# One expert per 32-column tile in the first layer of a mixture of experts

## The chip, the cores and the metric

The kernel runs on one core of a Trainium2 chip. The metric is the time in microseconds of one execution, the median of three runs. Lower is better. A core has TensorE (matmuls, which write into PSUM, 8 banks of 128 partitions x 512 f32), VectorE, ScalarE, GpSimd (POOL) and SyncE (SP), each with an instruction stream of its own; they wait for each other with semaphores.

## The reference

```
x = x + tanh(g_xattn) * xattn(layernorm(x), ctx)           # 16 batches, 1024 tokens, 512 features
x = x + tanh(g_ffn) * ffn(layernorm(x))
ffn:   grouped = x.reshape(b, s // 32, 32, d)              # 32 groups of 32 tokens
       logits  = einsum('bntd,des->bntes', grouped, Wc) + bc + tie     # 32 x 4 = 128 experts
       perm    = (logits == max over the 32 tokens)        # each expert takes one token of each group
       permuted        = einsum('bntd,bntes->bnesd', grouped, perm)    # the gather
       inner           = relu(einsum('bnesd,esdf->bnesf', permuted, W1) + b1)   # first layer, 512 -> 32
       result_permuted = einsum('bnesf,esdf->bnesd', inner, W2) + b2            # second layer, 32 -> 512
       result          = einsum('bnesd,bntes->bntd', result_permuted, perm)     # the scatter
```

Each of the 128 experts has its own W1 (512 x 32) and takes 32 tokens of a batch, one from each of the 32 groups.

## The kernel before

The program has two parts that follow each other. The attention part handles 32 half batches and leaves its result in `out`. The expert part (`experts`, from L1074) then goes through 16 batches, and the change touches only this part. It runs in f32.

TensorE's order for batch i stands in `tensor`. There is first one stretch, the **gather and first layer**: pieces n = 0 to 7, each one block of 128 features (n // 2) for one half of the tokens or of the experts (n % 2). `gather(i, n)` (L1398) picks tokens with 16 matmuls of 32 rows x 128 columns, four row tiles beside each other, into four banks: banks 4 to 7, or 0 to 3 for n = 1. ScalarE and VectorE copy these banks into `gat` (`copy`, L1285 and L1341). `inner(i, p)` (L1422) then multiplies: for each pair of experts one matmul with 64 columns of W1-side rows, so that the 64x64 result holds the two experts' products with both experts' tokens; half of each result is never used. All pieces add up in banks 0 to 3, which `bias` (L1413) has filled with b1 first. The pieces go in the order gather 0, 1, 2, bias, inner 0, gather 3, inner 1 and so on. In every second batch the pieces are taken in reverse.

Eight `relu` steps on ScalarE (`hidden`, L1291) take the useful quarter-rows of these banks into `hid`. After the stretch TensorE does the scatter of the batch before (`scatter`, 8 tiles), the second layer (`outer`, 8 steps of 4 bias matmuls and 16 matmuls on 32x32 tiles) and two transposes of the choice for the next batch (`route.chosen_T`, L208). ScalarE copies these into `sel` (L213), and the next gather needs them. VectorE's `swap` (L1339) transposes the second layer's result in `res` for the scatter.

Weights that don't stay in SBUF are loaded in quarters of 256 KB: W1 by SP (L1197, L1205), three pieces of W2 by ScalarE's queue (`load_second`, L1185), the last of them after the last piece of the first layer (`m_w1` step 7). POOL normalises the next batch's tiles (`route.normed`, L182) and adds the finished tiles to `out` (L1260); between the first four and the last four tiles it waits for the last W2 load.

Semaphore counts are kept by `Mark` objects; `m_gaA` and `m_gaV` count ScalarE's and VectorE's copies, `m_w1` the pieces of the first layer, `m_hr` the relus.

Of the kernel before, what the change touches and what calls it, by code (L numbers as in the profile page):

```python
# [17 lines left out]
P = 128  # L18
# [3 lines left out]
E, G = 128, 32  # L22
F = 32
# [1044 lines left out]
def experts(nc, top, ps, kept, d_kept, consts, ident, gate_f, xin, ring, d_ring, route, m_b2s, late_logits, logits_landed, w1_dram, w2_dram, out):  # L1068
# [7 lines left out]
    with st:  # L1076
# [19 lines left out]
        m_gaA, m_hr, m_evA = mark("gaA", 2 * C), mark("hr", 8), mark("evA", 8)  # L1096
        m_gaV, m_evV, m_tr, m_fin = mark("gaV", 2 * C), mark("evV", 8), mark("tr", 8), mark("fin", NT - 2)
# [9 lines left out]
        front = lambda n: 0 if n == 1 else 4  # L1107
# [40 lines left out]
        def gathered(n, g):  # L1148

            return (gat[:, n // 2 % 2, :].rearrange("p (e h g t) -> p h e g t", h=2, g=GT, t=TH)[:, n % 2, :, g],  # L1150
                    ps[:, front(n):front(n) + 4, :].rearrange("p g (t e) -> p e g t", t=TH)[:, :, g])
# [132 lines left out]
        def scalar(e):  # L1284
            def copy(i, n):  # L1285
                e.wait_ge(m_gap.sem, m_gap.at(i, n))
                room_for(e, i, n)
                o, v = gathered(n, slice(0, 2 if n < 2 else 3))
                e.activation(o, v, ACT.Copy).then_inc(m_gaA.sem, 1)  # L1289

            def hidden(i, j, p):  # L1291
                e.wait_ge(m_w1.sem, m_w1.at(i, p))
                o, v = relu(i, j, piece(i, p) % 2)
# [7 lines left out]
            for i in range(B):  # L1301
                if live(i):
# [31 lines left out]
        def vector(e):  # L1334
# [6 lines left out]
            def copy(i, n):  # L1341
                e.wait_ge(m_gap.sem, m_gap.at(i, n))
                room_for(e, i, n)
                o, v = gathered(n, slice(2 if n < 2 else 3, 4))
# [216 lines left out]
```

## Time and profile before

| | us |
|---|---|
| median of 3 runs | 1759.36 (1754.37 to 1762.72) |
| the profiled execution | 1774.67 |
| its span | 1772.9 |
| attention part, about | 0 to 884 |
| sixteen stretches of gather and first layer, in sum | 485.2 |

| engine | busy us | share |
|---|---|---|
| TensorE, matmuls | 1638.3 | 92% |
| TensorE, weight loads | 1147.6 | 65% |
| VectorE | 1296.2 | 73% |
| POOL | 854.9 | 48% |
| ScalarE | 736.4 | 42% |

The mean granted clock of TensorE is 0.979 of full speed. Matmuls overlap each other and the weight loads, so the busy time of TensorE is that of the union of its records, whose ends are modelled. The chain of waits that ended last is TensorE's for 57%, DMA's for 19%, VectorE's for 12%; for 5% of the span it holds "issue", time in which an engine waited for nothing that the profile shows.

### The profile page before, as it was taken

How to read it: one execution, taken by the hardware profiler on the slowest of the kernel's cores; microseconds unless marked ns; L12 is line 12 of the kernel's file. 1: busy time of each engine (PE TensorE's matmuls, PEld its weight loads, DVE VectorE, ACT ScalarE, POOL GpSimd, SP SyncE). 2: the span in 40 equal slices, each digit the busy share in tenths (PEclk: the TensorE clock that was granted, in tenths of full speed). 3: DMA queues.
4: the chain of work that ended last, by engine and by line, in shares of the span. 5: the costliest groups of instructions: out<-in, count | busy, mean ns of one | idle time of the engine just before them, and what ended most of it. 6: DMA issues, size and time to landing. Idle time of an engine off the chain costs nothing.

```text
span 1772.9 us, 51861 instructions
## 1 busy us (share of the span) xinstructions
PE 1638.3 (92%) x22488; PEld 1147.6 (65%) x22488; DVE 1296.2 (73%) x1886; ACT 736.4 (42%) x965; POOL 854.9 (48%) x1016
## 2 busy tenths in 40 slices
PE   7899999999999999999878999999988989998995
PEld 4677777777777777777656555666555666554663
DVE  5677777787777777777717777677777777776866
ACT  3532323233332333233234555454555554555552
POOL 3368777877778777877611222122222122222122
PEclk9999999999999999999989999999999999999997
DMA  7634545554454545454554887777888777878765
GB/s 273 171 98 148 172 142 176 156 164 159 148 189 159 167 145 177 155 165 148 185 188 141 214 216 212 210 204 201 223 212 213 214 209 198 208 204 226 213 170 157
DMA packets 180882, 324.81 MB, mean 183 GB/s; under 512 B 23344, under 2 KB 33328, under 8 KB 179248
## 3 DMA queue, kind: packets, MB, share of 16 engines
q1 hardware_dynamic: 135728, 239.68, 42.5%
q0 software_dynamic: 17280, 31.46, 11.0%
q10 hardware_dynamic: 27648, 50.34, 8.9%
q8 instruction: 179, 2.93, 0.7%
q14 instruction: 47, 0.39, 0.1%
HBM read 242.71 MB, written 78.71 MB: 181 GB/s over the span
## 4 chain that ended last, share of the span: by engine, by line
PE 57%; DMA 19%; DVE 12%; issue 5%; ACT 3%; POOL 2%; SPq 1%; ACTq 0%; POOLq 0%; DVEq 0%
PE ps L1435 12%; PE ps L899 10%; PE ps L946 10%; DMA xin<-out 7%; PE ps L1408 6%; DMA out<-xin 5%; PE ps L959 5%; PE ps L914 3%; PE ps L972 3%; DVE mx L694 2%; DMA gat<-in_W 2%; PE ps L1459 2%; DMA sel<-lg_scratch 2%; PE ps L933 2%; ACT lg L663 2%
## 5 line engine op out<-in xcount | busy, mean ns | idle before, releaser
L182 POOL TENSOR_SCALAR xin<-xin,r_all,nb_all 128x512 f32<-128x512 f32 x128 | 112.2, 880 | 524.7 <-DMA xin<-out 377.4
L1339 DVE STREAM_TRANSPOSE res<-res 128x2048 f32<-128x2048 f32 x128 | 292.1, 2295 | 0.1
L1289 ACT ACTIVATE gat<-ps 128x1536 f32<-128x1536 f32 (+1 forms) x128 | 170.9, 1344 | 235.4 <-PE ps L1408 235.2
L1355 DVE COPY res<-ps 128x1024 f32<-128x1024 f32 x128 | 156.7, 1225 | 85.3 <-PE ps L1459 66.2
L899 PE MATMUL ps<-xTh,qh 128*128 128x512 f32 x512 | 209.5, 409 | 5.0 <-DVE qs L711 1.4
L1408 PE MATMUL ps<-sel,xin 32*128 32x128 f32 x4096 | 157.2, 284 | 51.0 <-issue 25.7
L899 PE MATMUL ps<-xTh,ql 128*128 128x512 f32 x512 | 200.8, 392 | 0.0
L899 PE MATMUL ps<-xTl,qh 128*128 128x512 f32 x512 | 200.3, 391 | 0.0
L1345 DVE COPY gat<-ps 128x512 f32<-128x512 f32 (+1 forms) x128 | 104.1, 816 | 102.6 <-PE ps L1408 102.4
L1408 PEld LDWEIGHTS ps<-sel,xin 32*128 32x128 f32 x4096 | 131.9, 186 | 65.5 <-issue 38.9
L1299 ACT ACTIVATE res<-ps 128x1024 f32<-128x1024 f32 x128 | 131.0, 1024 | 101.0 <-PE ps L1459 90.4
L530 POOL TENSOR_TENSOR xTl<-xT,xTh 128x512 fp32r<-128x512 f32 x128 | 160.4, 1284 | 11.2 <-ACT xTh L595 11.2
L1260 POOL DMA_DIRECT2D out<-xin x120 | 119.0, 1049 | 95.8 <-DVE xin L1174 80.2
L946 PE MATMUL ps<-vw,pTh 128*128 128x512 f32 x512 | 164.2, 402 | 0.1
L543 POOL TENSOR_TENSOR qc<-qc,qs 128x512 f32<-128x512 f32 x64 | 82.8, 1294 | 162.9 <-DVE qs L711 162.9
L726 DVE TENSOR_TENSOR xin<-ps,xin 128x512 f32<-128x512 f32 x128 | 88.2, 689 | 67.2 <-PE ps L946 67.2
L710 DVE TENSOR_TENSOR qc<-ps,cos 128x512 f32<-128x512 f32 x128 | 86.9, 679 | 60.0 <-PE ps L899 59.9
L946 PEld LDWEIGHTS ps<-vw,pTh 128*128 128x128 f32 x512 | 94.1, 189 | 45.6 <-issue 25.2
L612 ACT ACTIVATE lx<-ps 128x512 f32<-128x512 f32 x32 | 19.1, 597 | 245.1 <-PE ps L959 245.1
L899 PEld LDWEIGHTS ps<-xTh,qh 128*128 128x128 f32 x512 | 96.6, 189 | 35.3 <-DVE qs L711 18.1
L663 ACT ACTIVATE lg<-lg,sc 128x256 f32<-128x256 f32 x128 | 58.2, 502 | 133.6 <-DVE lg L698 133.6
L1435 PE MATMUL ps<-gat,kept 128*64 128x64 f32 x3072 | 107.2, 229 | 6.3 <-issue 6.1
(156 smaller groups left out, 3335.2 us busy)
## 6 DMA issues: line engine op xcount, KB each, us to landing
gat<-in_W ACTq DMA_DIRECT2D x192, 256.0 KB, 5.1
xT<-in_xT SPq DMA_DIRECT2D x32, 1024.0 KB, 6.2
xin<-in_x SPq DMA_DIRECT2D x64, 512.0 KB, 3.8
out<-xin SPq DMA_DIRECT2D x64, 512.0 KB, 4.3
xin<-out SPq DMA_DIRECT2D x128, 256.0 KB, 4.1
xin<-in_W SPq DMA_DIRECT2D x128, 256.0 KB, 3.9
out<-xin POOLq DMA_DIRECT2D x120, 256.0 KB, 7.5
xT<-in_W SPq DMA_DIRECT2D x68, 256.0 KB, 4.6
```

The source lines that it names most:

```text
L182: e.tensor_scalar(self.xn[:, t, :], self.xn[:, t, :], self.r[:, i, t:t + 1], self.nb[:, i, t:t + 1], ALU.mult, ALU.add).then_inc(self.m_xn ...
L530: e.tensor_tensor(xTl[:, c, :], xT[:, c, :], xTh[:, c, :].bitcast(F32), ALU.subtract).then_inc(m_lo.sem, 1)
L899: last = e.matmul(ps[:, 2 + n % 2, :], a[:, c, n * DH:(n + 1) * DH], b[:, c, :], start=(k == 0), stop=(k == len(parts) - 1))
L946: last = e.matmul(ps[:, 5 + t % 2, :], a[:, t // 2, column:column + P], vw[:, u // 2 % 2, k, p, :], start=(m == 0), stop=(m == len(parts) ...
L1260: e.dma_start(batch(out, b, t, 1)[:, 0], tile_of(t), accum_op=ALU.add).then_inc(d_ys[t].sem, 16)
L1289: e.activation(o, v, ACT.Copy).then_inc(m_gaA.sem, 1)
L1299: e.activation(o, v, ACT.Copy).then_inc(m_evA.sem, 1)
L1339: e.transpose(v, v).then_inc(m_tr.sem, 1)
L1345: e.tensor_copy(o, v).then_inc(m_gaV.sem, 1)
L1355: e.tensor_copy(o, v).then_inc(m_evV.sem, 1)
L1408: last = e.matmul(ps[:, front(n) + g, t * E:(t + 1) * E], xn[r, h * TH + t, c * P:(c + 1) * P], sel[r, h * TH + t, :], start=True, stop=True)
L1435: last = e.matmul(ps[a * 64:(a + 1) * 64, q // 8, q % 8 * 64:(q % 8 + 1) * 64], first(i, p)[:, (e0 % 64) * F:(e0 % 64 + 2) * F], gat[:, c ...
```

## The change

In `inner` each expert gets a matmul of its own: 32 columns of weights in the column tile j = 0 to 3, its own 32 tokens as the moving rows, a 32x32 result without an unused part. Four column tiles stand beside each other, and 64 matmuls take the place of 32 in a piece. The results of all experts fit two banks (0 and 1) instead of four, so `bias` has two matmuls instead of four and waits for `sel` rather than for the copies, and `relu` has two steps of 128 partitions instead of eight of 32. The six banks 2 to 7 form a ring for the gathers: gather n takes four banks from 2 + (4n mod 6) on. `gathered(n, k)` copies two banks at a time; for n < 2 ScalarE takes the first two and VectorE the last two, as before, and from n = 2 on ScalarE takes both in two steps, where before it took three banks and VectorE one. VectorE's swaps no longer have copies between them, and the first stands ahead of copy 0. Two of the four loads of W2_MOVED[1] and all of W2_MOVED[2] move behind later steps of ScalarE's loop over the finished tiles.

```diff
-        front = lambda n: 0 if n == 1 else 4
+        front = lambda n, g: 2 + (4 * n + g) % 6
...
-        def relu(i, j, h):
-            return (hid(i)[j * F:(j + 1) * F].rearrange("p (s q) n -> p s q n", s=4)[:, 2 * h:2 * h + 2],
-                    ps[j * F:(j + 1) * F, 2 * h:2 * h + 2, :].rearrange("p s (q b n) -> p s q b n", b=2, n=NG)[:, :, :, j % 2])
+        def relu(i, h):
+            return hid(i)[:, h * Q // 2:(h + 1) * Q // 2].rearrange("p q n -> p (q n)"), ps[:, h, :]
...
+        def in_place(e, i, n, k):
+            if n < 2 and k:
+                e.wait_ge(m_gaV.sem, m_gaV.at(i, n))
+            else:
+                e.wait_ge(m_gaA.sem, m_gaA.at(i, n if n < 2 else 2 * n - 2 + k))
...
-                    for p in (2 * C - 2, 2 * C - 1):
-                        for j in range(4):
-                            hidden(i, j, p)
-                            if p % 2:
-                                load_second(e, i, W2_MOVED[1], j)
+                    hidden(i, 2 * C - 2)
+                    hidden(i, 2 * C - 1)
+                    for c in range(2):
+                        load_second(e, i, W2_MOVED[1], c)
...
-                    if live(i) and t < QUARTERS:
-                        load_second(e, i, W2_MOVED[2], t)
+                    if live(i) and t < 2:
+                        load_second(e, i, W2_MOVED[1], 2 + t)
+                    elif live(i) and t < 2 + QUARTERS:
+                        load_second(e, i, W2_MOVED[2], t - 2)
...
-                    if live(i):
-                        if k == 0:
-                            copy(i, 0)
-                        if k < 7:
-                            copy(i, k + 1)
                     if live(i - 1):
                         swap(i - 1, k)
+                    if live(i) and k == 0:
+                        copy(i, 0)
+                        copy(i, 1)
...
+                if n:
+                    in_place(e, i, n - 1, 0)
                 if n >= 2:
-                    k = 0 if n == 2 else n - 1
-                    e.wait_ge(m_gaA.sem, m_gaA.at(i, k))
-                    e.wait_ge(m_gaV.sem, m_gaV.at(i, k))
+                    in_place(e, i, n - 2, 1)
...
-                    for a in range(2):
-                        e0 = 4 * q + 2 * a
-                        last = e.matmul(ps[a * 64:(a + 1) * 64, q // 8, q % 8 * 64:(q % 8 + 1) * 64],
-                                        first(i, p)[:, (e0 % 64) * F:(e0 % 64 + 2) * F], gat[:, c % 2, e0 * NG:(e0 + 2) * NG],
+                    for j in range(4):
+                        e0 = 4 * q + j
+                        last = e.matmul(ps[j * F:(j + 1) * F, q // 16, q % 16 * NG:(q % 16 + 1) * NG],
+                                        first(i, p)[:, (e0 % 64) * F:(e0 % 64 + 1) * F], gat[:, c % 2, e0 * NG:(e0 + 1) * NG],
                                         start=False, stop=(c == C - 1), skip_group_check=True)
```

TensorE at the start of the second batch's stretch, before. `ps<-sel,xin` is a gather, `ps<-ident,b1r` the bias, `ps<-gat,...` a piece of the first layer with its weights in `xT`, `xin` or `kept`; the numbers are the result's shape and how many stand in a row.

```order
L1408 MATMUL ps<-sel,xin 128x128 x48
L1418 MATMUL ps<-ident,b1r 128x512 x4
L1435 MATMUL ps<-gat,xT 64x64 x32
L1408 MATMUL ps<-sel,xin 128x128 x16
L1435 MATMUL ps<-gat,xin 64x64 x32
L1408 MATMUL ps<-sel,xin 128x128 x16
L1435 MATMUL ps<-gat,kept 64x64 x32
```

The same place in the changed kernel:

```order
L1415 MATMUL ps<-sel,xin 128x128 x32
L1424 MATMUL ps<-ident,b1r 128x512 x2
L1415 MATMUL ps<-sel,xin 128x128 x16
L1441 MATMUL ps<-gat,xT 32x32 x64
L1415 MATMUL ps<-sel,xin 128x128 x16
L1441 MATMUL ps<-gat,xin 32x32 x64
L1415 MATMUL ps<-sel,xin 128x128 x16
L1441 MATMUL ps<-gat,kept 32x32 x64
```

The bias stands one gather earlier, and each piece has 64 matmuls in place of 32, between the same gathers.

ScalarE at the end of the second batch's stretch, before: `gat<-in_W` is a load of a quarter of W2, `gat<-ps 32x512` a relu, `xin<-ps,gate_f` a finished tile of the batch before.

```order
L1289 ACTIVATE gat<-ps 128x128x12 x6
L1185 DMA gat<-in_W 128x512 x4
L1294 ACTIVATE gat<-ps 32x512 x5
L1185 DMA gat<-in_W 128x512
L1294 ACTIVATE gat<-ps 32x512
L1185 DMA gat<-in_W 128x512
L1294 ACTIVATE gat<-ps 32x512
L1185 DMA gat<-in_W 128x512
L1294 ACTIVATE gat<-ps 32x512
L1185 DMA gat<-in_W 128x512 x3
L1176 ACTIVATE xin<-ps,gate_f 128x512
L1185 DMA gat<-in_W 128x512
```

And in the changed kernel:

```order
L1297 ACTIVATE gat<-ps 128x128x8 x14
L1192 DMA gat<-in_W 128x512 x4
L1302 ACTIVATE gat<-ps 128x512 x2
L1192 DMA gat<-in_W 128x512 x4
L1183 ACTIVATE xin<-ps,gate_f 128x512
L1192 DMA gat<-in_W 128x512
L1183 ACTIVATE xin<-ps,gate_f 128x512
L1192 DMA gat<-in_W 128x512
```

Fourteen copies of 128x128x8 take the place of two of that size and six of 128x128x12; two relus stand where eight stood; the last load of W2 stands behind the fourth finished tile, where it stood behind the second.

## Rows read from the trace of the kernel before

**Rows 1.** The page: busy us, share and instructions of each engine.

```profile
PE 1638.3 (92%) x22488; PEld 1147.6 (65%) x22488; DVE 1296.2 (73%) x1886; ACT 736.4 (42%) x965; POOL 854.9 (48%) x1016
```

**Rows 2.** TensorE's waits, 780 to 1773 us: us in total, times, longest.

```profile
PE ps L1408 <- issue: 25.7, 22, 2.2
...
PE ps L1435 <- issue: 9.7, 12, 1.7
...
PE ps L1418 <- DVE gat L1345: 5.0, 11, 0.5
...
PE ps L1454 <- ACT gat L1294: 4.5, 1, 4.5
```

**Rows 3.** Busy time by stretch: gather and first layer; the last row a scatter.

```profile
core 0: us, PE busy (x) PEld busy (x) DVE busy (x) ACT busy (x) POOL busy (x), PEclk, DMA share, GB/s
...
1049.40:1080.00 30.60, 26.97 (x780) 24.42 (x784) 24.20 (x16) 12.75 (x12) 5.29 (x7) 1.00 0.71 191
1102.20:1137.00 34.80, 30.03 (x780) 27.49 (x784) 24.84 (x17) 12.80 (x12) 5.18 (x7) 0.90 0.63 180
...
sum 485.20, PE 432.85 PEld 393.20 DVE 373.00 ACT 202.51 POOL 68.23; mean PE 27.05 PEld 24.57 DVE 23.31 ACT 12.66 POOL 4.26
...
1080.00:1087.00 7.00, 7.00 (x69) 1.86 (x68) 4.71 (x7) 6.15 (x11) 3.51 (x4) 1.00 0.94 284
```

**Rows 4.** TensorE in order of time: start, us, what, count, idle before.

```profile
1006.78 0.50 PE L1408 MATMUL ps<-sel,xin 32*128 32x128 f32 x7 [0.90 <-issue]
1007.21 2.08 PE L1435 MATMUL ps<-gat,xin 128*64 128x64 f32 x64
1009.23 1.17 PE L1408 MATMUL ps<-sel,xin 32*128 32x128 f32 x32
1010.33 0.92 PE L1435 MATMUL ps<-gat,kept 128*64 128x64 f32 x24
1011.64 0.74 PE L1435 MATMUL ps<-gat,kept 128*64 128x64 f32 x18 [0.39 <-issue]
```

**Rows 5.** The same view in the batch with the longest stretch.

```profile
1112.81 0.50 PE L1408 MATMUL ps<-sel,xin 32*128 32x128 f32 x6 [2.16 <-issue]
1113.24 3.63 PE L1435 MATMUL ps<-gat,xin 128*64 128x64 f32 x64
...
1126.26 0.94 PE L1408 MATMUL ps<-sel,xin 32*128 32x128 f32 x23
1129.13 0.60 PE L1408 MATMUL ps<-sel,xin 32*128 32x128 f32 x9 [1.92 <-issue]
```

**Rows 6.** 780 to 1773 us: instruction queue (packets, MB, share); instructions of each engine.

```profile
q8 instruction: 149, 2.44, 1.0%
...
780.00:1773.00 993.00, 880.75 (x18833) 576.85 (x18831) 706.74 (x675) 481.64 (x556) 284.85 (x343) 0.97 0.73 198
```

**Rows 7.** TensorE after a wait; then the instruction queue, 1059.65 to 1059.75.

```profile
1058.58 0.50 PE L1408 MATMUL ps<-sel,xin 32*128 32x128 f32 x7 [0.90 <-issue]
...
q8 instruction: 1, 0.02, 71.2%
```

**Rows 8.** The instruction queue, 1110.45 to 1110.55.

```profile
q8 instruction: 1, 0.02, 58.2%
```

**Rows 9.** Last scatter at full clock; matmuls of L1459, 1034.42 to 1034.50.

```profile
1759.31 1.96 PE L1486 MATMUL ps<-res,selT 128*32 128x128 f32 x64 [0.74 <-DVE res L1339]
...
1034.43 0.68 PE L1459 MATMUL ps<-kept,gat 32*32 32x512 f32 x11
```

**Rows 10.** ScalarE by form, 780 to 1773 us: count, busy us, mean ns, idle before.

```profile
L1289 ACT ACTIVATE gat<-ps 128x1536 f32<-128x1536 f32 x96 | 139.3, 1451 | 209.2 <-PE ps L1408 209.0
...
L1289 ACT ACTIVATE gat<-ps 128x1024 f32<-128x1024 f32 x32 | 32.3, 1023 | 26.2 <-PE ps L1408 26.2
```

**Rows 11.** TensorE in order of time: gathers 1 and 2 of a batch.

```profile
1050.95 2.27 PE L1408 MATMUL ps<-sel,xin 32*128 32x128 f32 x64 [0.33 <-POOL xin L182]
```

**Rows 12.** The last load of W2 on ScalarE's queue.

```profile
1031.88 0.78 ACTq L1185 DMA_DIRECT2D gat<-in_W  x1
```

More of the change, by code:

```diff
@@ L1095, in experts @@
         m_gap, m_w1, m_w2, m_sc = mark("gap", 2 * C), mark("w1", 2 * C), mark("w2", 8), mark("sc", NT)
[L1096 to L1097 removed]
+        m_gaA, m_hr, m_evA = mark("gaA", 4 * C - 2), mark("hr", 2), mark("evA", 8)
+        m_gaV, m_evV, m_tr, m_fin = mark("gaV", 2), mark("evV", 8), mark("tr", 8), mark("fin", NT - 2)
         d_last = mark("last", 4, 16)
@@ L1140, in second, with gathered @@
             return v.rearrange("p (k d) -> p k d", d=D)
-        def relu(i, j, h):
-            return (hid(i)[j * F:(j + 1) * F].rearrange("p (s q) n -> p s q n", s=4)[:, 2 * h:2 * h + 2],
-                    ps[j * F:(j + 1) * F, 2 * h:2 * h + 2, :].rearrange("p s (q b n) -> p s q b n", b=2, n=NG)[:, :, :, j % 2])
-        def gathered(n, g):
-            return (gat[:, n // 2 % 2, :].rearrange("p (e h g t) -> p h e g t", h=2, g=GT, t=TH)[:, n % 2, :, g],
-                    ps[:, front(n):front(n) + 4, :].rearrange("p g (t e) -> p e g t", t=TH)[:, :, g])
+        def relu(i, h):
+            return hid(i)[:, h * Q // 2:(h + 1) * Q // 2].rearrange("p q n -> p (q n)"), ps[:, h, :]
+        def gathered(n, k):
+            b = front(n, 2 * k)
+            return (gat[:, n // 2 % 2, :].rearrange("p (e h g t) -> p h e g t", h=2, g=GT, t=TH)[:, n % 2, :, 2 * k:2 * k + 2],
+                    ps[:, b:b + 2, :].rearrange("p g (t e) -> p e g t", t=TH))
+        def in_place(e, i, n, k):
[3 more added lines that the diff above has]
+                e.wait_ge(m_gaA.sem, m_gaA.at(i, n if n < 2 else 2 * n - 2 + k))
         def room_for(e, i, n):
@@ L1287, in copy, with hidden @@
                 room_for(e, i, n)
-                o, v = gathered(n, slice(0, 2 if n < 2 else 3))
-                e.activation(o, v, ACT.Copy).then_inc(m_gaA.sem, 1)
-            def hidden(i, j, p):
+                for k in range(1 if n < 2 else 2):
+                    o, v = gathered(n, k)
+                    e.activation(o, v, ACT.Copy).then_inc(m_gaA.sem, 1)
+            def hidden(i, p):
                 e.wait_ge(m_w1.sem, m_w1.at(i, p))
-                o, v = relu(i, j, piece(i, p) % 2)
+                o, v = relu(i, piece(i, p) % 2)
                 e.activation(o, v, ACT.Relu).then_inc(m_hr.sem, 1)
@@ L1343, in copy @@
                 room_for(e, i, n)
-                o, v = gathered(n, slice(2 if n < 2 else 3, 4))
+                o, v = gathered(n, 1)
                 e.tensor_copy(o, v).then_inc(m_gaV.sem, 1)
@@ L1407, in gather @@
                         r = slice(g * G, (g + 1) * G)
-                        last = e.matmul(ps[:, front(n) + g, t * E:(t + 1) * E], xn[r, h * TH + t, c * P:(c + 1) * P], sel[r, h * TH + t, :],
+                        last = e.matmul(ps[:, front(n, g), t * E:(t + 1) * E], xn[r, h * TH + t, c * P:(c + 1) * P], sel[r, h * TH + t, :],
                                         start=True, stop=True)
@@ L1412, in bias @@
             def bias(i):
-                e.wait_ge(m_gaA.sem, m_gaA.at(i, 1))
-                e.wait_ge(m_gaV.sem, m_gaV.at(i, 1))
-                for s in range(4):
-                    r = slice(s * G, (s + 1) * G)
-                    e.matmul(ps[:, s, :].rearrange("p (q n) -> p q n", q=8), b1r[r, :],
-                             ident[r, s * G + 8 * s:s * G + 8 * s + 8].unsqueeze(2).broadcast_to([G, 8, 2 * NG]),
+                e.wait_ge(m_sel.sem, m_sel.at(i, 1))
+                for h in range(2):
+                    r = slice(h * G, (h + 1) * G)
+                    e.matmul(ps[:, h, :].rearrange("p (q n) -> p q n", n=NG), b1r[r, :],
+                             ident[r, h * G + h * Q // 2:h * G + (h + 1) * Q // 2].unsqueeze(2).broadcast_to([G, Q // 2, NG]),
                              start=True, stop=False, skip_group_check=True)
@@ L1427, in inner @@
                 if p % 2 == 0:
-                    e.wait_ge(m_gaA.sem, m_gaA.at(i, p + 1))
-                    e.wait_ge(m_gaV.sem, m_gaV.at(i, p + 1))
+                    for k in range(2):
+                        in_place(e, i, p + 1, k)
                 for q in range(n % 2 * 16, n % 2 * 16 + 16):
@@ L1446, in outer @@
                 elif u == 0:
-                    e.wait_ge(m_hr.sem, m_hr.at(i, 7))
+                    e.wait_ge(m_hr.sem, m_hr.at(i, 1))
                 elif i:
@@ L1495, in tensor @@
                             gather(i, n)
-                        if n == 2:
+                        if n == 1:
                             bias(i)
```

3 lines of the change are left out of this document (1 added, 2 removed).

## Prediction

> **What bounds the kernel now.** I read the page's totals first [rows 1], then the waits of TensorE in the expert part [rows 2], then a table of that part's gather-and-first-layer stretches [rows 3], then the instructions around single waits [rows 4, 5]. TensorE is busy 92% of the span, so it looks like the bound, and the change halves its work in its costliest line. But "busy" hides what feeds it. In each of the 16 batches there is one stretch with 8 gathers and 8 first-layer pieces. The sixteen stretches sum to 485.2 us, 30.3 us each, with 27.05 us busy [rows 3]. The idle time there is mostly put down to "issue": 25.7 us in 22 waits before L1408 and 9.7 us in 12 before L1435 [rows 2]. "Issue" means that nothing which the profile shows was waited for.
>
> The counts say what it is. Between the wait that ended at 1006.78 and the one that ended at 1011.64 stand 7+64+32+24 = 127 matmuls and as many weight loads, 254 instructions [rows 4]. Between those that ended at 1112.81 and 1129.13 stand 6+64+32+64+32+64+32+64+23 = 381 matmuls [rows 5], with their weight loads 762, three times 254. Both waits cut a gather or a piece in its middle. The DMA view has a queue named "instruction", with 149 packets in the expert part [rows 6], where TensorE ran 18833+18831 = 37664 instructions, 253 per packet [rows 6]. With the few semaphore instructions, a packet of 16 KB is 256 instructions. So TensorE's program comes in by blocks of 256, and these waits are for the next block.
>
> How long one takes: a block began at 1058.58 and the next packet started in the tenth of a microsecond around 1059.7, 1.1 us later [rows 7]; a packet that started at 1110.5 ended its wait at 1112.81, 2.3 us later [rows 5, 8]. Together that is 3.45 us for 256 instructions at the least, if the packet for a block is asked for only when the block ahead of it begins. That it is asked so late I infer: before 1112.81 TensorE stood dry for 2.16 us, and the packet that ended this started 2.3 us ahead, when it had just run dry. Call this time R. A stretch has 8x64 + 16 + 8x128 = 1552 instructions, 6.06 blocks; without a wait a block takes about 256/192 x (1.10+2.02) = 4.2 us, from a gather (1009.23 to 1010.33) and a piece (1007.21 to 1009.23) [rows 4]. The sixteen stretches cross 97 block limits and show 34 such waits, so R is below 4.2 us at two in three, and where it shows it is 4.2 + 35.4/34 = 5.2 us. Mean: 1/3 x 5.2 + 2/3 x 3.8 (middle of 3.45 and 4.2) = 4.3 us. **The kernel today sits just at the rate at which TensorE's program arrives.**
>
> **The first layer.** Each f32 matmul of the code is two matmuls and two weight loads in the trace (32 in the order, 64 in [rows 4]). A piece goes from 32 matmuls of 64x64 to 64 of 32x32, from 128 to 256 instructions. The array's share falls: a column tile streams 32 columns per matmul instead of 64 and four tiles work beside each other instead of two. The nearest rows are the last scatter's, 128 rows by 32 columns: 64 matmuls that stream 128 columns each in 1.96 us at the full clock [rows 9]; a quarter of the columns gives a quarter of that, for 128 matmuls 0.98 us. Against 2.02 us this saves 1.0 us a piece, 8.3 us a stretch, 133 us in all, if the program arrives.
>
> It does not. A stretch now has 512 + 8 + 2048 = 2568 instructions, 10.03 blocks. A block is consumed in 256/320 x (1.10+0.98) = 1.7 us, far below R. Of the ten limits crossed, the first finds its block there (the second layer before it is slow enough), nine wait in full: 9R, and 1.9 us for the two partial blocks at the ends. The DMA share of 0.69 in such a stretch (0.63 to 0.71 in the rows shown, [rows 3]) should fall, as the same bytes are spread over a longer batch, so I take R = 4.1, a little below today's 4.3: 9 x 4.1 + 1.9 = 38.8 us against 30.3, **+8.5 us a batch, +136 us**. Bounds: R = 3.45 gives 33.0 us, +43 us; R = 5.0 (30.3/6.06, every limit as slow as the mean block today) gives 46.9 us, +266 us.
>
> [...]
>
> **Clock.** A wait of 2.16 us was followed by a piece that took 3.63 us instead of 2.08 [rows 4, 5], at half the granted clock (mean 0.90 in that stretch [rows 3]). With a wait of about 4.1-1.7 = 2.4 us at each limit the low clock will be common. Inside the stretch this costs nothing: a block at half clock takes 3.4 us, still below R. At its end the scatter starts low at times: between 0 and 3.5 us lost there (half of the 7.0 us that it takes [rows 3]); I take 1.0 us a batch, +16 us.
>
> **Ring of six banks, split copies.** Gather 1 now waits for ScalarE's copy of gather 0, which takes 1.02 us [rows 10], where it had banks of its own. Behind it wait the bias and the first piece. Today gather 1 waits 0.33 us for POOL's tile anyway [rows 11]; so 0.7 us more at most, and a block on its way uses that time: 0. From the third gather on ScalarE makes both copies, 2 x 1.02 instead of 1.45 us [rows 10], for a piece every 38.8/8 = 4.9 us: hidden; without the fetch it would just equal the 2.1 us of gather and piece. VectorE loses six copies a batch and has its swaps in a row. The first swap stands ahead of copy 0 and holds it about 0.6 us; the same cover: 0.
>
> **Bias and relu.** The bias no longer waits for the copies (5.0 us of waits in all [rows 2]) and two relus on 128 partitions replace eight on 32. In 15 batches the scatter covers the relus. In the first nothing does: 4.5 us of L1454 waiting on ScalarE [rows 2], of which about 4 go. The bias's 5.0 us are spent on program arrival anyway. Together -4 us.
>
> **Loads of the second layer.** The last load to `gat` went out at 1031.88, after the second finish [rows 12]; POOL waits for its landing before it prepares the tiles of the next batch's gather 1. It now stands behind four finishes, but ScalarE is out of its relus some 2.5 us sooner; the last goes out within 0.5 us of where it did: 0, between -8 and +8 us.
>
> **Sum**: 136 + 16 - 4 = +148 us. The profiled execution would take 1774.67 + 148 = 1923 us; the median of the runs is 15 us below the profiled one, so 1759 + 148 = **1907 us**.
>
> **Rivals.**
> A. The program keeps up (blocks are asked for sooner when TensorE runs fast). Then gather and piece are bound by the array and, from the third on, evenly by ScalarE: -133 us of work, and the waits stay: 1626 us. For: two thirds of today's limits show no wait. Against: no stretch consumed a block faster than about 4 us, so nothing shows a shorter R. It decides in favour of faster as soon as R is below (30.3-1.9)/9 = 3.15 us, below the 3.45 that the rows show. Chance 0.08.
> B. Each f32 instruction costs what it costs now whatever its size: 64 matmuls in 2.02 us are 31.5 ns each, 32 of the gather in 1.10 us 34 ns [rows 4]. A piece takes 4.04 us, a block 4.0, level with R: stretch 1284 x 31.5 ns + waits as today = 42.7 us, +198 us, with the rest 1970 us. Against: 11 matmuls of L1459 on different tiles start within 0.07 us, and the last scatter does 64 in 1.96 us including its tail [rows 9]. Chance 0.10. [...]
> C. R falls to its floor, since the DMA engines are emptier, and the clock holds: +43 - 4 = 1798 us. Chance 0.12.
>
> **Numbers.** Forecast 0.70, near 1907 (R from 3.6 to 4.8: 9R+1.9 = 34.3 to 45.1 us, +64 to +237, with the rest 1835 to 2008). The range takes in the upper part of C and most of B: 1820 to 1995. About 0.5% is what a measurement of this kernel tells from no change. Faster by more: A and a little of C, 0.09. Same: 0.03. Slower: 0.88.
>
> **What would show it.** About 13 packets of the instruction queue a batch instead of 9; waits put down to "issue" at nearly every 254 instructions of the stretch, most of 2 us or more; stretches of 37 to 41 us while the pieces' own busy time, at the full clock, is near 1 us; a lower mean clock. Wrong if stretches are below 30 us (A), or if pieces run on without a break at 4 us (B).

## The result, and the profile after

The changed kernel takes 1971.67 us (median of 4 runs, 1970.13 to 1976.01) against 1756.86 us before (4 runs on the same chip, 1753.55 to 1762.72). The ratio is 1.122, with a 95% interval of 1.118 to 1.126. The profiled executions have spans of 1970.2 and 1772.9 us, 197.3 us apart, and the readings below account for these. The medians are 214.8 us apart: the profiled execution of the kernel before, at 1774.67 us, lies 18 us above its median, the one of the changed kernel (1972.03 us) at its median.

The page of the changed kernel: the span, each engine's busy time, the clock that TensorE was granted in 40 slices, and the instruction queue. [rows 1] has the same line of before.

```profile
span 1970.2 us, 67911 instructions
...
PE 1632.4 (83%) x30616; PEld 1119.4 (57%) x30616; DVE 1233.0 (63%) x1790; ACT 732.7 (37%) x965; POOL 855.7 (43%) x1016
...
PEclk9999999999999999996898789978987997798788
...
q8 instruction: 242, 3.96, 0.8%
```

TensorE runs 8128 more matmuls and as many more weight loads. Its busy time is unchanged (1632 against 1638 us), and its share has fallen from 92% to 83%: so what came on top of the span is idle time. In the expert part, the right half of the clock line, the clock is no longer at 9 throughout: 0.85 on average from 780 us on, where [rows 6] has 0.97.

TensorE's waits in the expert part (780 to 1970 us): us in total, how often, longest. They answer to [rows 2].

```profile
PE ps L1441 <- issue: 195.3, 116, 4.1
PE ps L1415 <- issue: 54.4, 25, 3.7
PE ps L1415 <- ACT gat L1297: 22.9, 32, 1.1
PE ps L1415 <- ACT sel L213: 10.6, 12, 0.9
```

L1441 is the first layer, L1415 the gather. Before gather and first layer, waits in which nothing shown was waited for have gone from 35.4 us in 34 to 249.7 us in 141. The third line is the ring's wait for ScalarE's copies, new with the change.

The stretches of gather and first layer, read in the columns of [rows 3]: one batch, the sum of all sixteen, then one scatter and the sum of all fifteen scatters.

```profile
1076.30:1119.20 42.90, 27.27 (x1288) 23.95 (x1292) 20.42 (x11) 14.60 (x16) 3.71 (x5) 0.75 0.56 153
...
sum 686.80, PE 413.19 PEld 359.31 DVE 309.15 ACT 233.38 POOL 61.08; mean PE 25.82 PEld 22.46 DVE 19.32 ACT 14.59 POOL 3.82
...
1119.20:1127.20 8.00, 8.00 (x68) 1.76 (x57) 4.05 (x6) 3.36 (x5) 3.53 (x4) 0.86 0.73 168
...
sum 131.50, PE 131.50 PEld 37.02 DVE 59.20 ACT 60.05 POOL 52.73; mean PE 8.77 PEld 2.47 DVE 3.95 ACT 4.00 POOL 3.52
```

A stretch takes 42.9 us on average (686.8/16) where it took 30.3. A scatter takes 8.8 us where it mostly took 7.0. The same cut through both traces accounts for the whole difference:

| | before | after | difference |
|---|---|---|---|
| 16 stretches of gather and first layer | 485.2 | 686.6 | +201.4 |
| from a stretch's end to the second layer, 15 scatters among it | 113.7 | 132.3 | +18.6 |
| second layer | 227.6 | 209.2 | -18.4 |
| between the second layer and the next gather | 28.8 | 28.6 | -0.2 |
| start of the first stretch; what follows the last second layer | | | -2.0; -2.0 |
| sum | | | +197.4 |

TensorE in order of time in the batch at 1076 us. Columns: start, duration, line, what, count, and in brackets the idle time before it and its cause.

```profile
1081.00 1.17 PE L1415 MATMUL ps<-sel,xin 32*128 32x128 f32 x32 [0.30 <-ACT gat L1297]
1082.10 1.13 PE L1441 MATMUL ps<-gat,xT 128*32 128x32 f32 x108
1085.92 0.38 PE L1441 MATMUL ps<-gat,xT 128*32 128x32 f32 x20 [2.69 <-issue]
1086.23 1.17 PE L1415 MATMUL ps<-sel,xin 32*128 32x128 f32 x32
1087.33 1.27 PE L1441 MATMUL ps<-gat,xin 128*32 128x32 f32 x75
1089.76 0.97 PE L1441 MATMUL ps<-gat,xin 128*32 128x32 f32 x53 [1.15 <-issue]
...
1109.37 0.97 PE L1441 MATMUL ps<-gat,kept 128*32 128x32 f32 x56 [0.15 <-issue]
1110.20 1.18 PE L1441 MATMUL ps<-gat,xin 128*32 128x32 f32 x72
1113.14 0.66 PE L1441 MATMUL ps<-gat,xin 128*32 128x32 f32 x54 [1.76 <-issue]
...
1118.26 0.98 PE L1441 MATMUL ps<-gat,xT 128*32 128x32 f32 x56 [3.79 <-issue]
1119.03 8.26 PE L1479 MATMUL ps<-res,selT 128*32 128x512 f32 x64
```

Between the waits that ended at 1085.92 and 1089.76 stand 20+32+75 = 127 matmuls, and with their weight loads 254 instructions, as in [rows 4]. The array is quick: 108 matmuls of the first layer in 1.13 us, at most 10.5 ns each. Then it stands for 2.69 us. The instruction queue answers to [rows 7, 8]: nothing moves on it from 1113.15 to 1115.85 us, and one packet starts in the tenth of a microsecond behind that.

```profile
q8 instruction: 1, 0.02, 60.0%
```

So the block that began at 1113.14 had the next one's packet start only 2.8 us later, and that block began at 1118.26, 2.4 us after its packet.

### The profile page after: what moved, and what is told of

Read it like the earlier page. It is cut to its first block, busy times and chain, and to the rows that moved or that the text cites. A ratio compares the mean times of both kernels' runs of the same rounds, so it can differ in the third digit from the quotient of the medians.

```text
span 1970.2 us, 67911 instructions
## 1 busy us (share of the span) xinstructions
PE 1632.4 (83%) x30616; PEld 1119.4 (57%) x30616; DVE 1233.0 (63%) x1790; ACT 732.7 (37%) x965; POOL 855.7 (43%) x1016
## 4 chain that ended last, share of the span: by engine, by line
PE 66%; issue 15%; DVE 8%; ACT 4%; DMA 4%; POOL 1%; SPq 0%; ACTq 0%; POOLq 0%
PE ps L1441 11%; PE ps L1415 9%; PE ps L899 9%; PE ps L946 9%; PE ps L1479 6%; PE ps L1465 5%; PE ps L959 4%; PE ps L914 3%; PE ps L972 2%; PE ps L1460 2%; DVE mx L694 2%; DMA gat<-in_W 2%; ACT gat L1297 2%; PE ps L933 1%; ACT lg L663 1%
## 5 line engine op out<-in xcount | busy, mean ns | idle before, releaser
L182 POOL TENSOR_SCALAR xin<-xin,r_all,nb_all 128x512 f32<-128x512 f32 x128 | 122.9, 966 | 586.7 <-DMA xin<-out 441.5
L1297 ACT ACTIVATE gat<-ps 128x1024 f32<-128x1024 f32 x224 | 218.9, 1021 | 310.3 <-PE ps L1415 310.3
L1415 PE MATMUL ps<-sel,xin 32*128 32x128 f32 x4096 | 187.7, 320 | 90.9 <-issue 54.4
L1267 POOL DMA_DIRECT2D out<-xin x120 | 128.7, 1121 | 232.6 <-DVE xin L1181 218.0
L1415 PEld LDWEIGHTS ps<-sel,xin 32*128 32x128 f32 x4096 | 156.4, 217 | 116.3 <-issue 56.3
L1441 PE MATMUL ps<-gat,xin 128*32 128x32 f32 x6144 | 85.4, 215 | 87.3 <-issue 87.1
L191 DVE SCALAR_TENSOR_TENSOR sel<-sel,bcol,tie 128x512 f32<-128x512 f32 x16 | 12.5, 782 | 207.0 <-DMA sel<-lg_scratch 207.0
L1479 PE MATMUL ps<-res,selT 128*32 128x512 f32 x960 | 136.5, 721 | 0.0
L1441 PEld LDWEIGHTS ps<-gat,xin 128*32 128x32 f32 x6144 | 74.5, 127 | 100.0 <-issue 96.8
L1441 PE MATMUL ps<-gat,kept 128*32 128x32 f32 x6144 | 88.0, 220 | 48.4 <-issue 48.2
```

The costliest lines, as they stand in the source:

```text
L182: e.tensor_scalar(self.xn[:, t, :], self.xn[:, t, :], self.r[:, i, t:t + 1], self.nb[:, i, t:t + 1], ALU.mult, ALU.add).then_inc(self.m_xn ...
L1267: e.dma_start(batch(out, b, t, 1)[:, 0], tile_of(t), accum_op=ALU.add).then_inc(d_ys[t].sem, 16)
L1415: last = e.matmul(ps[:, front(n, g), t * E:(t + 1) * E], xn[r, h * TH + t, c * P:(c + 1) * P], sel[r, h * TH + t, :], start=True, stop=True)
L1441: last = e.matmul(ps[j * F:(j + 1) * F, q // 16, q % 16 * NG:(q % 16 + 1) * NG], first(i, p)[:, (e0 % 64) * F:(e0 % 64 + 1) * F], gat[:, c ...
L1479: last = e.matmul(ps[g * G:(g + 1) * G, 4 + t % 4, :].rearrange("p (d2 d1) -> p d2 d1", d1=2), s[:, g * G:(g + 1) * G], r[:, 8 * (t // TH) ...
```

## The experiments

The first two ask which part of the change costs the time.

**Only the first layer's tiles** (the kernel before with this one edit; its four accumulator banks, eight relus and gather banks stay):

```
-                    for a in range(2):
-                        e0 = 4 * q + 2 * a
-                        last = e.matmul(ps[a * 64:(a + 1) * 64, q // 8, q % 8 * 64:(q % 8 + 1) * 64],
-                                        first(i, p)[:, (e0 % 64) * F:(e0 % 64 + 2) * F], gat[:, c % 2, e0 * NG:(e0 + 2) * NG],
+                    for j in range(4):
+                        e0, o = 4 * q + j, q % 8 * 64 + j % 2 * NG
+                        last = e.matmul(ps[j * F:(j + 1) * F, q // 8, o:o + NG],
+                                        first(i, p)[:, (e0 % 64) * F:(e0 % 64 + 1) * F], gat[:, c % 2, e0 * NG:(e0 + 1) * NG],
```

> The kernel before with one edit: in the first layer one expert per 32-column tile, its own 32 rows alone; four accumulator banks, bias, eight relus, copies and gather banks stay as they were. Theory 1 (the program arrives in blocks of 256 instructions, one in 4.1 us when TensorE is dry, as in the changed kernel's 141 blocks): a stretch has 2576 instructions. Its first three gathers and the bias take 5.3 us as in the kernel before, the other 9.2 blocks 4.1 us each: 43 us, less about 1 us for the copies that gather 1 need not wait for. That is 41 to 43 us a stretch and 1940 to 1975 us in all, nearly the whole loss of the change. Theory 2 (the loss comes from the ring of six banks and the copies split in two on ScalarE): this kernel has neither, so it is no slower than before, and with half the array's work 1630 to 1760 us. Theory 3 (a matmul instruction costs some 31 ns whatever its size): pieces of 4 us without a break in them, 1940 to 1980 us, told from theory 1 by the rows only: under theory 1 about 108 matmuls in 1.1 us and then a wait.

Measured: 1958.97 us, ratio 1.114 (1.109 to 1.120). Its longest kind of wait, then the sum of its stretches:

```profile
PE ps L1435 <- issue: 224.4, 113, 4.3
```

```profile
sum 679.50, PE 415.71 PEld 364.10 DVE 378.37 ACT 213.08 POOL 66.80; mean PE 25.98 PEld 22.76 DVE 23.65 ACT 13.32 POOL 4.17
```

The tile edit alone makes 202.1 of the 214.8 us (1958.97 and 1971.67 against 1756.86). Everything else of the change (bank ring, split copies, merged relus, the order of swaps and copies, the later loads) together makes the other 12.7 us, of which 7.3 us lie in the stretches (686.8 - 679.5). The two intervals touch (1.109 to 1.120, 1.118 to 1.126), so that their cost is small is sure, and its size is not.

**The same in every second step** (`if p % 2:` the four small matmuls, `else:` the two of before):

> As tiles_only, but only in every second piece of the first layer (the odd steps); the others keep 64 columns for two experts. 2064 instructions in a stretch. Theory 1: 5.3 us for the first three gathers and the bias, then 7.2 blocks of 4.1 us: 35 us, 4.5 us more than the 30.3 us of before in each of 16 batches, 1757 + 72 = about 1830 us, roughly a third of the full loss, since before the change the array was still the slower half of the time. Theory 3 (31 ns for each matmul): half the full loss, about 1860 us. If the program always arrived in time, 1757 - 65 = 1690 us.

Measured: 1863.94 us, ratio 1.059 (1.055 to 1.064); half the added instructions cost about half the time (107 of 202 us). L1436 is the line of the small matmuls. Its waits, then TensorE in one such piece:

```profile
PE ps L1436 <- issue: 124.4, 60, 4.3
...
1082.98 1.23 PE L1436 MATMUL ps<-gat,kept 128*32 128x32 f32 x120
1087.39 0.33 PE L1436 MATMUL ps<-gat,kept 128*32 128x32 f32 x8 [3.18 <-issue]
```

By its time alone the run would speak for theory 3: it lies 4 us from the 1860 us of theory 3 and 34 us above the 1830 us of theory 1. The rows speak against theory 3: 120 small matmuls in 1.23 us, then a wait of 3.18 us, where theory 3 has 4 us without a break. Theory 1 had its sizes too small. Stretches are 36.9 us, above its 35: a stretch has 2064 instructions, 8.06 blocks, and behind a block's start the next packet came later here (1.85 us on average, against 1.66 in the changed kernel). Waits for the program number 76, not one at each of the eight limits of 16 stretches: at the others TensorE itself was the slower side.

**Half of the first layer's matmuls left out** of the changed kernel:

```
-                    for j in range(4):
+                    for j in range(q % 2, 4, 2):
```

> The changed kernel, with half of the first layer's matmuls left out (two of the four column tiles for each q, alternating), so half of the experts' first layer is not computed. A piece has 128 instructions again, as before the change, at a quarter of its array work. Theory 1: a stretch starts with 5.8 us as in the changed kernel and has 5.2 blocks of 4.1 us left: 27 us, against 42.8 in the changed kernel, so 1972 - 250 = about 1720 us. Theory 3 (31 ns for each matmul): pieces of 2.0 us as before, about 1757 us. A theory that puts the loss on the ring and the split copies keeps it: above 1850 us.

Measured: 1766.21 us, ratio 1.004 (1.002 to 1.007), where 1720 had been expected. It has the instruction count of the kernel before, with matmuls a quarter as large in its first layer (128x32 by 32 columns for 128x64 by 64). Its waits for the program before the first layer, then its stretches:

```profile
PE ps L1441 <- issue: 91.7, 47, 6.6
```

```profile
sum 453.00, PE 295.00 PEld 248.12 DVE 299.39 ACT 233.12 POOL 48.69; mean PE 18.44 PEld 15.51 DVE 18.71 ACT 14.57 POOL 3.04
```

They are 28.3 us each, close to the 27 of the expectation: 18.4 us with TensorE busy in them, 28.3 us of time. With the count of before and far less work the stretch is only 2 us shorter (28.3 against 30.3), so most of it follows the count and not the work. Not all of its idle time is the program's: waits for it before gather and first layer are 108.4 us in 60, and waits of a gather for ScalarE's copies have grown from 22.9 us in 32 in the changed kernel to 42.6 us in 73. Where a block is there in time, ScalarE's two copies now set the pace (a wait of about 0.45 us before each gather). The stretches are 234 us shorter than the changed kernel's; the rest of the miss stands elsewhere. The 15 scatters take 134.5 us (109.3 before, 131.5 in the changed kernel), as 14 of them start at a low clock (0.50 to 0.64 in their first microsecond, where the kernel before has 1.00), and the first batch's second layer takes 31.3 us where the changed kernel takes 16.0, 9.8 of it one wait for ScalarE, of the same origin as the one told below for the kernel before.

The next three look for what makes a block take 4.1 us.

**Eight loads of W1 a batch left out of the changed kernel** (the ring pieces read the resident ones):

```
-            return middle if n == W1_MIDDLE else ring[p % 2 if p < 2 else 1 - p % 2]
+            return middle if n == W1_MIDDLE else kept[:, n % 3, :]
...
-                    for k, c in ((0, 0), (0, 1), (1, 0), (1, 1), (1, 2), (1, 3), (0, 2), (0, 3)):
-                        load_end(i, k, c)
```

> The changed kernel without the eight loads of 256 KB a batch that bring the two ring pieces of W1; those pieces of the first layer use weights that are kept, so their values are not the reference's, and the work of every engine is as before. It asks how much of the 4.09 us for a block of instructions is other transfers in the way of its packet. After a wait the next packet starts 1.05 to 2.77 us later (mean 1.62 over 126 blocks), and its arrival takes 2.46 us from there. Theory 1 with contention: the mean start falls to 1.1 to 1.3 us while the ring loads are gone, so a block takes 3.6 to 3.8 us, and 9.2 blocks in 16 stretches save 40 to 70 us: 1900 to 1930 us. Without contention (the 4.09 us are the packet's own way): 1960 to 1975 us. If TensorE's pieces had waited for W1 rather than for their program, far more would go, down to 1757 us.

Measured: 1953.57 us, ratio 1.109 (1.106 to 1.112); 18 us less than the changed kernel, where 40 to 70 had been expected, a miss. The period of a block falls from 4.09 to 3.97 us only. **The same left out of the kernel before**:

> The kernel before with the same loads left out (ring pieces of W1 take kept weights, values not the reference's). Its 34 waits on the program sum to 35 us. Theory 1: with a block in 3.6 to 3.8 us, less than the 4.2 us that TensorE needs for one, most of these waits go: 25 to 35 us less, 1720 to 1735 us, and the sum of its 'issue' waits before gathers and pieces falls below 15 us. If those waits have another cause than the packets: 1750 to 1760 us.

Measured: 1716.74 us, ratio 0.975 (0.973 to 0.978), 40 us less, better than expected. TensorE's waits put down to issue before gather and first layer fall from 35.4 us in 34 [rows 2] to 8.2 in 10 (7.2 at the gather, below, and 1.0), and its stretches from 485.2 us [rows 3] to 442.4:

```profile
PE ps L1406 <- issue: 7.2, 9, 1.6
```

```profile
sum 442.40, PE 419.45 PEld 383.63 DVE 377.13 ACT 202.99 POOL 74.41; mean PE 26.22 PEld 23.98 DVE 23.57 ACT 12.69 POOL 4.65
```

The pair says two things. The waits of before come from packets that other transfers delay: they go with those transfers, and the traces show the delay itself. With the block limits counted out from the waits, the next packet of the kernel before starts 1.4 us after a block's start where the DMA share in that first microsecond is under 0.3 (25 blocks), and 3.0 us after it where the share is over 0.7 (39 blocks). Part of the 42.8 us between the two sums of stretches may not be this effect, since the profiled execution of the kernel before lies 18 us above its median. And once every block is waited for, as in the changed kernel, traffic is a small part of the 4.1 us: most of it remains with the DMA share of the expert part at 0.54 instead of 0.62.

**One load of W1 under way instead of two** (the kernel before, with `c >= 1` and `[c - 1]` in place of `c >= 2` and `[c - 2]` in both waits ahead of these loads):

> The kernel before, all work kept, with SP's twelve W1 loads of a batch let out one at a time instead of two (each waits for the one ahead of it). Leaving eight of them out took 43 us and most of the waits for the program away. If it is the depth of transfers ahead of the instruction packet that delays it, shorter queues give part of this: the 35.4 us of 'issue' waits fall to 15 to 28 us, 1735 to 1750 us, which would beat both kernels. If it is their number, or the other transfers, nothing changes: 1752 to 1762 us. If the loads then come late, pieces wait for W1: above 1765 us.

Measured: 1942.91 us, ratio 1.105 (1.102 to 1.108): the last branch of the expectation, by far more than it had. The waits for the program went (1.2 us in 4 before gathers, none before the first layer), but the loads came late:

```profile
PE ps L1435 <- DMA xin<-in_W: 85.5, 22, 7.1
...
PE ps L1474 <- DVE xin L1174: 75.3, 17, 6.5
```

Stretches of 35 us ask for a block every 5.8 us only, so this run doesn't tell whether the depth of the queue is what delays a packet.

The remaining four are on the changed kernel's side effects.

**Gather 1 with banks of its own** (`front` gives it banks that gather 0 doesn't use; the bias waits instead):

```
-        front = lambda n, g: 2 + (4 * n + g) % 6
+        front = lambda n, g: g - 2 if n == 1 and g > 1 else 2 + (4 * n + g) % 6
...
-                if n:
+                if n > 1:
```

> The changed kernel with gather 1's last two banks moved from banks 2 and 3, which gather 0's copy must leave first, to banks 0 and 1, so that gather 1 follows gather 0 without a wait; the bias then waits for VectorE's copy of gather 1. All else as in the changed kernel. The changed kernel waits 22.9 us in all for ScalarE's copies before gathers, 1.13 us of it a batch before gather 1. If these waits lie on the path (no block of instructions is on its way at the stretch's start): 12 to 18 us less, 1955 to 1960 us. If the program's arrival covers them, as I had forecast: within 3 us of 1971 us.

Measured: 1976.67 us, ratio 1.123 (1.120 to 1.125), no gain. The wait moved on to the bias, which now needs the banks back:

```profile
PE ps L1424 <- DVE gat L1354: 30.9, 16, 2.5
```

So it doesn't tell what the ring's waits cost; the comparison with the tile edit alone does, above.

**Scatter tiles among the last two pieces.** Scatter matmuls are few and long (64 in the 8.0 us of the batch shown), so they could run while blocks are on their way. Six of the tiles were moved there:

```
+                between = []
+                if live(i - 1) and i < B and p >= 2 * C - 2:
+                    between = [3 * (p - 2 * C + 2) + t for t in range(3)]
...
+                    if q % 16 in (4, 8, 12) and between:
+                        scatter(i - 1, between.pop(0))
...
-                for t in range(NT):
+                for t in range(6, NT):
```

> The changed kernel, with six of the eight scatter tiles of the batch before moved up between the matmuls of the first layer's last two pieces (three in each); nothing is added or left out. Theory 1: TensorE waits there for its program for 1 to 4 us a block, so 6 tiles of 0.9 to 1.1 us run in time that was idle: 5 to 7 us less in each of 15 batches, 75 to 105 us, 1870 to 1895 us. Theory 3 (the pieces themselves take the time): nothing is idle, the sum stays, 1960 to 1975 us. VectorE's swaps must be over by then: the last must end before the seventh piece begins, otherwise part of the gain is lost in a wait for VectorE.

Measured: 1965.09 us, ratio 1.118 (1.112 to 1.124), a miss by 70 us. L1484 is the scatter. Its waits, then TensorE at the end of a stretch:

```profile
PE ps L1446 <- issue: 135.0, 98, 3.5
...
PE ps L1484 <- ACT xin L1183: 44.3, 15, 3.7
```

```profile
1117.73 0.47 PE L1446 MATMUL ps<-gat,xT 128*32 128x32 f32 x32
1120.85 3.30 PE L1484 MATMUL ps<-res,selT 128*32 128x512 f32 x16 [2.64 <-ACT xin L1183]
```

Of the 249.7 us of waits for the program 56 went (135.0 are left before the first layer, 52.4 before gathers, 6.3 before the scatter), and 44 us of a new wait came: ScalarE, which empties the scatter's banks, was still at the relus and loads ahead of it in its own order. A second version puts four of ScalarE's finishes between its two relus:

```
                     hidden(i, 2 * C - 2)
+                    for t in range(2, 6):
+                        if live(i - 1) and i < B:
+                            finish(e, i - 1, t)
                     hidden(i, 2 * C - 1)
```

> As scatter_between, with ScalarE's finishing of tiles 2 to 5 moved ahead of its second relu and of its loads of W2, so that the last two scatter tiles find their banks free. In scatter_between these two waited for ScalarE 44.3 us in all (15 times, up to 3.7 us). Theory 1 (the moved tiles ran in waits for the program, and the gain was given back in this new wait and in a low clock behind it): 30 to 60 us less than scatter_between, 1905 to 1935 us. Theory 3 (the tiles found no idle time): no change, 1960 to 1970 us.

Measured: 1961.0 us, ratio 1.116 (1.111 to 1.121), a miss again: ScalarE issued its seven loads in a row ahead of the last finishes, and `PE ps L1468 <- ACT xin L1183` stood at 39.5 us in 15. A third version issues the first four of those loads ahead of the second relu, and the other four behind the finishes:

```
-                    hidden(i, 2 * C - 1)
-                    for c in range(2):
+                    for c in range(QUARTERS):
                         load_second(e, i, W2_MOVED[1], c)
+                    hidden(i, 2 * C - 1)
...
-                    if live(i) and t < 2:
-                        load_second(e, i, W2_MOVED[1], 2 + t)
-                    elif live(i) and t < 2 + QUARTERS:
-                        load_second(e, i, W2_MOVED[2], t - 2)
+                if live(i):
+                    for c in range(QUARTERS):
+                        load_second(e, i, W2_MOVED[2], c)
```

> As scatter_between2, with ScalarE's loads for the fourth W2 piece put ahead of its second relu and those for the last W2 piece behind its finishing of tiles 6 and 7. In scatter_between2 the second layer's second step waited 39.5 us in all for the last finished tile (15 times), because ScalarE issued seven loads in 4.3 us ahead of it. Theory 1: that wait goes, 25 to 40 us less, 1920 to 1935 us, and 35 to 50 us below the changed kernel. If the time comes back once more, it must be as another named wait behind the last piece; theory 3 (no idle time in the pieces): no change, 1958 to 1968 us.

Measured: 1945.42 us, ratio 1.106 (1.102 to 1.110), 26 us below the changed kernel and 10 above what was expected. From the start of the last piece but one to the second layer it takes 14.04 us (1107.83 to 1121.87) where the changed kernel took 17.02 (1110.20 to 1127.22). Its first and last rows:

```profile
1107.83 0.46 PE L1448 MATMUL ps<-gat,xin 128*32 128x32 f32 x32
...
1121.87 0.51 PE L1467 MATMUL ps<-b2s,rowk 32*128 32x512 f32 x4 [1.56 <-ACT gat L1302]
```

Long matmuls laid over the waits win some of the loss back, 3 us in this batch, and a new wait for ScalarE's second relu (1.56 us here) takes part of it. No version that does all the work came near the kernel before.

## Why the prediction was right, and where its terms were not

The forecast was 1907 us, +148, with 1820 to 1995 as its range, and slower at 0.88. The kernel is slower, by the mechanism that the forecast named, and inside the range, but 65 us above the middle.

**The mechanism holds.** Waits put down to issue number 141 against 34, in the stretches nearly always 254 to 256 instructions apart or twice that, and the tile edit alone brings nearly all of the loss. The packets rose as said: 212 in the expert part against 149 [rows 6], 63 more, 4 a batch. Below is the instruction queue from 780 to 1970 us.

```profile
q8 instruction: 212, 3.47, 1.2%
```

**The time of a block, R = 4.1 us, was right.** From the first wait for the program in a stretch to the last there are 132 blocks in the 16 stretches of the changed kernel. Their mean period is 4.09 us, and 125 of them end in a wait. In these 125 the next packet starts 1.66 us after the block (1.05 to 3.45; the 2.77 in the expectation of the run with fewer loads isn't the longest), and the next block begins 2.46 us after that. The floor of 3.45 us from one pair of rows each [rows 7, 8] was the early end of the first part. That the forecast hit 4.1 is partly luck. The 4.3 us that it took for the kernel before rests on the middle of an interval, 3.8 us, for two thirds of the blocks, which no row showed, and the 0.2 us less were a guess. Read from the trace of before in the same way, a packet starts 2.3 us after its block on average, which with 2.4 us to the next block makes 4.7 us: the forecast had the figure of before too low and its fall too small, and the two errors cancel.

**The ends of a stretch were the term that failed.** The prediction gave 9R and 1.9 us for the two partial blocks, pricing these at the mean rate of a block, 1.7 us. In the batch shown, the first block limit is crossed without a wait at 1081.34 (counted back 128 matmuls from 1085.92), nine waits later it is 1118.26: 36.9 us, or 9 x 4.10, as forecast. But 5.0 us lie ahead of the first limit and 0.9 behind the last, 5.9 instead of 1.9. Ahead of the first limit stand gathers, whose 64 instructions take 1.10 us where the first layer's 216 take 1.13, and the ring's waits. The next rows show this start in another batch, 5.7 us until the first layer begins:

```profile
1141.75 1.17 PE L1415 MATMUL ps<-sel,xin 32*128 32x128 f32 x32 [0.93 <-ACT sel L213]
1144.05 1.17 PE L1415 MATMUL ps<-sel,xin 32*128 32x128 f32 x32 [1.13 <-ACT gat L1297]
1145.05 1.02 PE L1424 MATMUL ps<-ident,b1r 32*128 32x512 f32 x4
1146.37 1.17 PE L1415 MATMUL ps<-sel,xin 32*128 32x128 f32 x32 [0.30 <-ACT gat L1297]
1147.47 1.16 PE L1441 MATMUL ps<-gat,xT 128*32 128x32 f32 x113
```

4.0 us a batch are 64 us, and all sixteen stretches bear this out: 686.8 us, where 16 times 38.8 are 621. That 64 is so near the 65 us by which the forecast missed the median is chance. The two profiles lie 197 us apart, 49 more than the 148 of the forecast: these 64 and 6 of the clock, less some 22 us that were not foreseen (below). The other 15 us of the 65 come from the median: the forecast took it to lie 15 us below the profiled execution again, as before the change, and it lies at it.

**The ring's waits, priced at 0, failed on their reason.** "A block on its way uses that time" is wrong in most stretches: the block for the first limit is already there, and the next seems to be asked for only when that limit is crossed (in the 125 blocks that end in a wait, no packet starts less than 1.05 us after the block). A wait ahead of it delays all that follows. In five of the sixteen (first wait for the program after 110 to 135 matmuls) the limit falls on the stretch's start, and there a block is on its way, as forecast. The price is 1.13+0.30 us a batch, 22.9 us of such waits in all, of which the 0.33 us [rows 11] and the bias's wait [rows 2] were there before. The net is small: with the edits other than the tiles taken away, the stretches were 7.3 us shorter in all.

**The clock was a little under-sized.** The forecast was +16 us, and 22 came. In their first microsecond all fifteen scatters are granted a clock of 0.50, where before all had 1.00, and as a whole 0.72 to 0.88, where fourteen of the fifteen had 1.00. The 15 scatters take 131.5 us instead of 109.3, and 109.3 holds one of 12.0 us. Against the usual 6.9 to 7.0 of before [rows 3] the mean of 8.8 us is 1.8 us more, 27 us in all. That one odd scatter gives 5 back.

**Bias and relu, -4 us, was right in the first batch**: from its stretch's end to the second layer 0.7 us instead of 4.5. **Not foreseen** was another 13.5 us there: the first batch's second layer takes 16.0 us instead of 29.5. In the kernel before, ScalarE and VectorE stood ahead of their first copies of the second layer's results until the attention part's last store of logits had landed, at 925.3 us, 8.5 us after the second layer had begun; then ScalarE issued four loads first. VectorE, then TensorE:

```profile
925.50 2.36 DVE L1355 COPY res<-ps 128x1024 f32<-128x1024 f32 x2 [19.15 <-DMA lg_scratch<-lx]
...
928.38 0.80 PE L1454 MATMUL ps<-b2s,rowk 32*128 32x512 f32 x4 [6.20 <-ACT res L1299]
...
937.77 0.80 PE L1454 MATMUL ps<-b2s,rowk 32*128 32x512 f32 x4 [4.59 <-issue]
```

In the changed kernel that store landed at 925.5 us too, but the longer stretch has covered it: the second layer begins at 928.36. The last wait, 4.59 us for the program, isn't there either. I had not read the first batch apart from the others. The sum, 136 + 64 + 22 - 4 - 13.5, is 205 us; the second layer's other 4.9 us and 4 us at both ends bring it near to the 197 of the profiles.

**The rivals.** Rival A, that the program keeps up, is refuted: stretches are 42.9 us, not below 30. The first stretch shows how little of the program stands ready ahead of its use. TensorE comes from the slow attention part, with 6927 matmuls and weight loads in the 720 us from 60 to 780 us, 26.6 us for every 256, so there is time to bring more than one block ahead:

```profile
882.77 1.17 PE L1415 MATMUL ps<-sel,xin 32*128 32x128 f32 x32 [0.35 <-DVE xin L726]
...
888.50 1.30 PE L1441 MATMUL ps<-gat,xT 128*32 128x32 f32 x128
889.73 1.16 PE L1415 MATMUL ps<-sel,xin 32*128 32x128 f32 x28
892.05 0.49 PE L1415 MATMUL ps<-sel,xin 32*128 32x128 f32 x4 [1.16 <-issue]
892.47 1.26 PE L1441 MATMUL ps<-gat,xin 128*32 128x32 f32 x124
896.87 0.32 PE L1441 MATMUL ps<-gat,xin 128*32 128x32 f32 x4 [3.14 <-issue]
```

Its first wait for the program comes after 512 instructions (32+32+4+32+128+28 matmuls with their weight loads), one block limit later than its start; the next comes 256 later. One block ahead was there, and not a second: on the instruction queue TensorE's packets of 16 KB start at 846.3, 881.5 and 889.5 us, and none in the 35 us between the first two.

Rival B, 31 ns for each instruction whatever its size, gave 1970 us, the measured time almost to the microsecond, and is refuted all the same: 108 matmuls took 1.13 us. By it pieces would run 4 us without a break, and waits would stay as they were. Only the rows tell the two apart, not the time. A whole piece, 128 matmuls, takes 1.30 us in the row above. Forecast was 0.98; that error costs nothing, since the array is waiting for its program anyway. Rival C, R at its floor of 3.45 us, is refuted by 4.09 us; even with less traffic it was 3.97 us.

## To carry to other kernels

Count the instructions of a stretch before cutting a matmul into smaller ones. In this kernel each f32 matmul of the code is two matmuls and two weight loads, and where the stretch would run through more than about 256 of these in 4 us (a block took 4.09 us here), the program's arrival is the bound and the array's gain is lost. When such a stretch is priced, price its start apart: what happens there before the first block limit is mostly not covered by any wait (5.0 us in the batch shown).

## What the runs showed of the hardware

- A block of 256 instructions of TensorE takes 4.09 us to come when every one is waited for: about 63 instructions a microsecond (256/4.09). In the 125 such blocks no packet started less than 1.05 us after the block ahead had begun, so the next seems to be asked for only then.
- Other DMA traffic delays single packets: in the kernel before they start 1.4 us after the block where the DMA share is under 0.3 and 3.0 us after it where it is over 0.7. With eight loads a batch fewer the kernel before loses 27 of its 35 us of such waits and 40 us of its time, but where every block is waited for, as in the changed kernel, only 18 us.
- Matmuls of 128 rows by 32 columns that go round four column tiles take at most 10.5 ns each (108 in 1.13 us, the last one's own time included), a third of the 31.5 ns of the 128x64 ones (64 in 2.02 us [rows 4]).
- Of the two parts of the 4.09 us, the first varies from 1.05 to 3.45 us, and traffic is part of the reason: it is 1.4 us on average where the DMA share in the block's first microsecond is under 0.3 (50 blocks) and 2.0 us where it is over 0.7 (41 blocks), and 1.44 us with eight loads a batch fewer. What makes up the rest of it, and the 2.46 us of the second part, stays open.
